# A GRU, two attentions and a mixture of experts on one core: gate inputs formed inside the recurrence, expert results stored by token and choice

## The reference

```python
def cell(h, x):                       # GRU, run over 512 steps for 4 sequences
    gi = x @ W_ih + b_ih
    gh = h @ W_hh + b_hh
    i_r, i_z, i_n = jnp.split(gi, 3, axis=-1)
    h_r, h_z, h_n = jnp.split(gh, 3, axis=-1)
    r = sigmoid(i_r + h_r); z = sigmoid(i_z + h_z)
    n = tanh(i_n + r * h_n)
    h_new = (1.0 - z) * n + z * h
...
x = x + differential_attention(GRU(cond_2048, x))   # causal, then a filter over frequencies, RMS norm
x = x + moe(attention(modulated_norm(x, cond_2048)))
...
# moe, over all 2048 tokens as one list: 64 experts, 6 choices a token
topk_w, topk_idx = jax.lax.top_k(softmax(xf @ gate_w.T), 6)
# pos: place of a choice within its expert; choices with pos >= CAP = 128 are dropped
gx = xp[buf_tok]                                       # 64 experts x 128 slots x 512
g, u = jnp.split(gx @ gate_up_proj, 2, axis=-1)        # inner size 192
eo = (silu(g) * u) @ down_proj * buf_w
routed = zeros.at[buf_tok].add(eo)                     # sum over a token's kept choices
out = routed + silu(xf @ sg.T) * (xf @ su.T) @ sd.T
```

## Time and profile before

| | |
|---|---|
| median of 3 runs | 4338.63 us (4338.46 to 4352.77) |
| the profiled execution | 4372.42 us, span 4370.6 us |
| gate inputs | 0 to 193 us |
| recurrence | 193 to 2070 us |
| attentions and filter | 2070 to about 3520 us |
| routing | about 3520 to 3792 us |
| experts | 3792 to 4217 us |
| combination | 4217 to 4370.6 us |
| busy, share of the span | TensorE 85%, VectorE 52%, ScalarE 32%, GpSimd 12% |

### The profile page before, as it was taken

The page is one execution under the profiler, slowest core; times in us unless marked ns, Lnnn a source line. Parts: engine busy times, 40 slices in busy tenths (PEclk is TensorE's granted clock), DMA queues, the critical chain, the costliest instruction groups (busy, mean ns, idle before and its releaser), DMA issues. The chain is left out here.

```text
span 4370.6 us, 166686 instructions
## 1 busy us (share of the span) xinstructions
PE 3724.0 (85%) x68215; PEld 2390.4 (55%) x68215; DVE 2284.5 (52%) x6296; ACT 1383.8 (32%) x4235; POOL 520.7 (12%) x1081
## 2 busy tenths in 40 slices
PE   8988888888888888888899999689999989688840
PEld 4477777777777777777344344244333344344420
DVE  2255555555555555555577777435666633222225
ACT  1133333333333333333344444224444411011100
POOL 0000000000000000000222222000000024200036
PEclk9999999999999999999999999899999889799975
DMA  3130000000000000000111110101211112278868
GB/s 102 48 136 0 0 0 0 0 0 0 0 0 0 0 0 0 0 0 6 61 52 43 41 50 17 70 29 52 67 50 50 52 68 72 66 251 265 265 200 203
DMA packets 136990, 253.11 MB, mean 58 GB/s; under 512 B 22135, under 2 KB 69379, under 8 KB 135012
## 3 DMA queue, kind: packets, MB, share of 16 engines
q1 hardware_dynamic: 97188, 157.86, 11.1%
q0 software_dynamic: 21056, 52.52, 4.3%
q10 hardware_dynamic: 18688, 41.96, 3.2%
HBM read 147.89 MB, written 62.92 MB: 48 GB/s over the span
## 5 line engine op out<-in xcount | busy, mean ns | idle before, releaser
L303 PE MATMUL gru_pr<-ahead,h 128*4 128x128 f32 x16384 | 556.7, 274 | 193.8 <-DVE h L384 193.8
L303 PEld LDWEIGHTS gru_pr<-ahead,h 128*4 128x4 f32 x16384 | 338.8, 88 | 399.7 <-DVE h L384 331.0
L303 PE MATMUL gru_pn<-ahead,h 128*32 128x128 f32 x16384 | 541.8, 273 | 0.0
L303 PE MATMUL gru_pz<-ahead,h 128*4 128x128 f32 x16384 | 541.7, 273 | 0.0
L303 PEld LDWEIGHTS gru_pn<-ahead,h 128*32 128x32 f32 x16384 | 458.4, 110 | 1.4
L303 PEld LDWEIGHTS gru_pz<-ahead,h 128*4 128x4 f32 x16384 | 438.0, 87 | 8.8
L331 ACT ACTIVATE gru_rn<-gru_pre 128x16 f32<-128x16 f32 x512 | 119.6, 234 | 704.6 <-DVE gru_pre L366 704.6
L364 DVE STREAM_TRANSPOSE gru_tr<-gru_pr 128x128 f32<-128x128 f32 x512 | 162.2, 317 | 335.1 <-PE gru_pr L303 335.1
L279 POOL COPY gru_pick<-ident 128x4 f32 x512 | 95.9, 187 | 1651.3 <-PE gru_pz L294 1645.9
L883 DVE TENSOR_REDUCE da_mx<-da_ps 128x2 f32<-128x1024 f32 (+3 forms) x256 | 201.2, 817 | 132.5 <-PE da_ps L576 132.5
L377 DVE STREAM_TRANSPOSE gru_tz<-gru_pz 128x32 f32<-128x32 f32 (+1 forms) x1024 | 195.1, 229 | 119.1 <-PE gru_pz L303 119.1
(11 more groups left out here) (281 smaller groups left out, 5418.8 us busy)
## 6 DMA issues: line engine op xcount, KB each, us to landing
ahead<-in_L_ffn_gate_up_proj SPq DMA_DIRECT2D x64, 768.0 KB, 9.2
ex_wd<-in_L_ffn_down_proj ACTq DMA_DIRECT2D x64, 384.0 KB
xg<-gru_zeros SPq DMA_DIRECT2D x4, 4096.0 KB
ex_xg<-xg ACTq DMA_DIRECT2D x64, 256.0 KB
eo<-ex_eo POOLq DMA_DIRECT2D x64, 256.0 KB
ahead<-wide SPq DMA_DIRECT2D x15, 1024.0 KB
ahead<-xnT SPq DMA_DIRECT2D x15, 1024.0 KB
da_wg<-ahead SPq DMA_DIRECT2D x45, 256.0 KB
```

The source lines that it names most:

```text
L303: last = nc.tensor.matmul(rows(j), of(c), whh[:, c, g, j, :], start=(c == 0 and start), stop=(c == KD - 1))
```

## The change

The inputs of the r and n gates are formed in the first stage for the first 32 time steps only (8 column groups of 4 products, 128x128). The others are formed within the recurrence: in each step but the last 32, TensorE does one 128x128 product for the block of 32 steps that follows, between the bias of n and the wait for h. Four such products are one column group; VectorE adds the bias and moves it to `giT` ahead of every fourth step, and GpSimd copies the group's columns of `W_ih` to a tile of its own, `wst`. `x` is kept transposed in `wide`, where each step's h takes the place of the inputs already used, and the second sequence is no longer held back for `W_ih`. The attention's weights come in the last 32 steps.

Each row of `xg` becomes 528 wide: beside the token's 512 values it carries the number of the token's first choice and its 6 experts; an empty slot has a million there. In the expert stage VectorE finds from these the row `token * 6 + choice` of each slot, and GpSimd stores the expert's rows to these places of a new tensor `yk` (12288 rows, cleared beforehand) with an indirect transfer, which leaves out empty slots. The combination then loads a tile's 6 rows a token, 12 KB in one piece for a partition, with plain transfers on SyncE's and ScalarE's queues in turn; it has no gather.

```diff
+                    transpose_x(b, k)
+            pe.wait_ge(w_spread, 3 * KD)
+            pe.wait_ge(xT_ready, B * KD)
+            for c in range(NG):
+                if c >= 2:
+                    pe.wait_ge(gi_out, c - 1)
+                for k in range(KD):
+                    last = nc.tensor.matmul(pg[:, c % 2, 0:B * 32], wih[:, k, c * P:(c + 1) * P], xT[:, k, :, 0:32], start=(k == 0), stop=(k == KD - 1))
                 last.then_inc(gi_psum, 1)
-
-            pe.wait_ge(ident_in, 16)
-            for k in range(KD):
-                transpose_x(0, k)
-            pe.wait_ge(w_spread, 3 * KD)
-            for b in range(B):
-                pe.wait_ge(xT_ready, (b + 1) * KD)
-                for c in range(NG):
-                    gate(b, c)
-                    if b < B - 1 and c in (3, 4, 5, 6):
-                        transpose_x(b + 1, c - 3)
...
+            sp.wait_ge(zero_set, 2)
+            R = 16
+            xg = t.xg_dram.rearrange("(n r p) d -> n p r d", r=R, p=P)
+            for n in range(SLOTS // (R * P)):
+                sp.dma_start(xg[n], zeros[:].broadcast_to([P, R, XW])).then_inc(cleared, 16)
+            yk = t.yk_dram.rearrange("(n r p) d -> n p r d", r=R, p=P)
+            for n in range(CHOICES // (R * P)):
+                sp.dma_start(yk[n], zeros[:, :, 0:D].broadcast_to([P, R, D])).then_inc(cleared, 16)
+            sp.wait_ge(cleared, 16 * (SLOTS // (R * P) + CHOICES // (R * P)))
+
+            sp.wait_ge(gi_psum, (NBL - 1) * NG)
...
+            with pool.Fori(0, NBL - 1) as kb:
+                block_of_z(kb)
+                with pool.Fori(0, NG) as c:
+                    for k in range(KD):
+                        if k == 2:
+                            pool.wait_ge(gi_out, kb * NG + c + 1)
+                            nc.gpsimd.tensor_copy(wst[:], wih[:, :, bass.ds(c * P, P)]).then_inc(wst_ready, 1)
+                        pick_step(kb, c * KD + k, k)
...
+            def next_gate_input(kb, c, k):
+                if k == 0:
+                    pe.wait_ge(gi_out, kb * NG + c + 1)
+                    pe.wait_ge(wst_ready, kb * NG + c + 1)
+                last = nc.tensor.matmul(pgi[:, 0:P], wst[:, k, :], xT[:, k, :, bass.ds(kb * 32 + 32, 32)],
+                                        start=(k == 0), stop=(k == KD - 1))
+                if k == KD - 1:
+                    last.then_inc(gi_psum, 1)
+
+            with pe.Fori(0, NBL - 1) as kb:
+                with pe.Fori(0, NG) as c:
+                    for k in range(KD):
+                        s = kb * 32 + c * KD + k
+                        add_z_input(s, k % 2)
+                        add_bias(s)
+                        next_gate_input(kb, c, k)
+                        step(s, k % 2)
...
+            def move_gate_input(kb, c):
+                dve.wait_ge(gi_psum, kb * NG + c + 1)
+                nc.vector.tensor_tensor(t.giT[:, bass.ds(kb * 32 + 32, 32), bass.ds(c * B, B)], pgi[:, 0:P].rearrange("p (b t) -> p t b", b=B),
+                                        t.gi_bias[:, 0, bass.ds(c, 1)].unsqueeze(2).broadcast_to([P, 32, B]), ALU.add).then_inc(gi_out, 1)
+
+            with dve.Fori(0, NBL - 1) as kb:
+                with dve.Fori(0, NG) as c:
+                    for k in range(KD):
+                        if k == 0:
+                            dve.wait_ge(gi_out, kb * NG + 1)
+                        if k == KD - 1:
+                            move_gate_input(kb, c)
+                        step(kb * 32 + c * KD + k, k % 2)
...
+                nc.vector.tensor_copy(yb[:, y, :, D], base[:]).then_inc(S["noted"], 1)
+                nc.vector.tensor_copy(yb[:, y, :, D + 1:D + 1 + K], ef[:].rearrange(k24, k=K)).then_inc(S["noted"], 1)
+                dve.wait_ge(S["noted"], b * 2 + 2)
+                nc.vector.tensor_scalar(base[:], base[:], float(K * T), None, ALU.add).then_inc(S["base_set"], 1)
+                dve.wait_ge(S["base_set"], b * 1 + (TT + 2))
...
+                    wait(pool, dest_ready, q, u + 1)
                     wait(pool, eo_ready, q, u + 1)
-                    nc.gpsimd.dma_start(t.eo_dram[bass.ds((q * U + u) * CAP, CAP), :], eo[:, u % 2, :]).then_inc(stored[u % 2], 16)
+                    pool.sem_inc(tick, 1)
+                    nc.gpsimd.indirect_dma_start(
+                        out=t.yk_dram, out_offset=bass.IndirectOffsetOnAxis(ap=dest[:, u:u + 1], axis=0),
+                        in_=eo[:, u % 2, :], in_offset=None, bounds_check=CHOICES - 1, oob_is_err=False).then_inc(stored[u % 2], 16)
...
+            def destinations(q, u):
+
+                v = u % U
+                wait(dve, ecur_set, q, u + 1)
+                nc.vector.scalar_tensor_tensor(hit[:], xg[:, v, D + 1:D + 1 + K], ecur[:, 0:1], kvec[:], op0=ALU.is_equal, op1=ALU.mult).then_inc(hit_done, 1)
+                wait(dve, hit_done, q, u + 1)
+                nc.vector.tensor_reduce(nth[:], hit[:], AX, ALU.add).then_inc(nth_done, 1)
+                nc.vector.tensor_scalar(ecur[:], ecur[:], 1.0, None, ALU.add).then_inc(ecur_set, 1)
+                wait(dve, nth_done, q, u + 1)
+                nc.vector.tensor_tensor(dest[:, v:v + 1], xg[:, v, D:D + 1], nth[:], ALU.add).then_inc(dest_ready, 1)
...
+        def loads_and_stores(queue, turn):
+            def load(n):
+                queue.dma_start(got[:, n % R, :, :].rearrange("p k d -> p (k d)"), rows[n]).then_inc(loaded[n % R], 16)
+
+            for n in range(turn, R, 2):
+                load(n)
+            for n in range(turn, NTILE, 2):
+                queue.wait_ge(summed, n + 1)
+                if n + R < NTILE:
+                    load(n + R)
+                queue.dma_start(out_t[n * P:(n + 1) * P, :], acc[:, n % R, :]).then_inc(stored[n % R], 16)
```

More of the change, by code:

```diff
@@ L30 @@
 SLOTS = E * CAP
+XW = D + 16
+CHOICES = B * T * K
 I = 192
@@ L183, in spread_w @@
                                               src.rearrange("p (j c i) -> p c j i", c=KD, j=KD)).then_inc(w_spread, 1)
-            for k in range(KD):
-                copy_x(0, k)
-            for k in range(KD):
-                spread_w(k)
+            for b in range(B):
+                for k in range(KD):
+                    copy_x(b, k)
+                    if b == 0:
+                        spread_w(k)
             dve.wait_ge(b_in, 16 * (4 * KD))
@@ L323, in _, with step @@
             act.wait_ge(set_up, 6)
-            with act.Fori(0, T) as s:
+            def step(s, kb):
                 gi = t.giT[:, bass.ds(s, 1), :].rearrange("p o c -> p (o c)")
+                act.wait_ge(gi_out, kb * NG + 1)
                 nc.scalar.activation(rn[:, :, 3], gi[:, ST:2 * ST], ACT.Copy).then_inc(gin_ready, 1)
@@ L336, in _ @@
                     nc.scalar.activation(cb(d1[:, part.start * B:part.stop * B, 2]), tz[:, part, 0:B], ACT.Sigmoid).then_inc(z_act, 1)
+            with act.Fori(0, NBL) as kb:
+                with act.Fori(0, 32) as n:
+                    step(kb * 32 + n, kb)
         @block.vector
@@ L1815, in _ @@
             nc.vector.tensor_copy(before[:], lf[:]).then_inc(S["ready"], 1)
+            nc.vector.tensor_reduce(above[:], lf[:], AX, ALU.add).then_inc(S["above_done"], 1)
+            dve.wait_ge(S["above_done"], 1)
+            for tt in range(TT):
+                nc.vector.tensor_scalar(base[:, tt:tt + 1], above[:], -float(K), float(K * (tt * P + P - 1)), ALU.mult, ALU.add).then_inc(S["base_set"], 1)
+            nc.vector.memset(yb[:, :, :, D:XW], 0.0).then_inc(S["base_set"], 1)
+            dve.wait_ge(S["base_set"], TT + 1)
             for k in range(KD):
@@ L2078, in round_of @@
                         copy_x(q, u + 1, first)
+                        if not first or u == U - 1:
+                            v = (u + 1) % U
+                            dve.wait_ge(stored[v % 2], q * (16 * U // 2) + (16 * ((u + 1) // 2 + 1) - 16 * U // 2))
+                        destinations(q, u + 1)
                     if not first or u:
@@ L2129, in _ @@
                     dve.wait_ge(stored[n % R], 16 * (n // R))
+                dve.wait_ge(loaded[n % R], 16 * (n // R + 1))
                 src = t.x1[:, n, :]
                 for k in range(K):
-                    dve.wait_ge(gathered[n % R][k], 16 * (n // R + 1))
                     if k:
```

144 lines of the change are left out of this document (65 added, 79 removed).

## The result

The changed kernel takes 4226.99 us (median of 4 runs, 4223.8 to 4241.51) against 4338.55 us before: ratio 0.9743, interval 0.9718 to 0.9768, 112 us faster. I had forecast 4183 us, 156 us faster, with a range of 4145 to 4240: the time lies in the whole range and outside the forecast's own, 4160 to 4205. The profiled execution has a span of 4227.2 us.

The account below looks back on a forecast made before the run. Bounds differed by stage: TensorE in gate inputs and the recurrence's closed chain, DMA largely in experts, GpSimd's indirect transfers in the combination. Terms -97 + 5 + 4 - 15 - 53 = -156 us gave 4183; own range 4160 to 4205, whole 4145 to 4240.

Parts of the forecast that it names:

- Gate inputs, -97: First stage: z inputs start at about 40 us in place of 137.8, 97 us less; ends -90 and -102.
- Recurrence, the product hidden: Each step's full-width product, 0.45 to 0.52 us, fits TensorE's 0.55 us pause before h; without cover 216 us.
- the small things: Recurrence loop: +5 us allowed for the product and all small things; other end +48 us.
- Rival 1: Recurrence: the full-width product doesn't fit in the pause, 0.10 us a step, 48 us, giving 4231 us; 14%.
- rival 2: Recurrence: GpSimd's copies to `wst` stop a VectorE scan, 120 x 0.32 = 38 us, giving 4221 us; 9%.
- Routing, +4: Routing stage: VectorE's small operations and waits before slots are written, plus setting up, add 4 us; ends +1 and +7.
- Experts, -15: Expert stage: fewer stored rows relieve DMA, new small operations stay hidden, 15 us less; ends -31 and +10.
- Rival 5: Expert stage: indirect stores cost there what the combination's gather did, 43 us, giving 4241 us; 3%.
- Combination, -53: Combination: plain loads replace gathers, VectorE's sums set the pace, 94 us in place of 147, 53 us less.
- rival 3: Combination: bound by DMA at 249 GB/s, 28 us more than forecast, giving 4211 us; 12%.

Follow-up runs that it names:

- g_twice: Changed kernel with each recurrence step's full-width product issued twice, the extra one to a PSUM bank nobody reads: 4334.39 us, ratio 0.9922.
- g_none: Changed kernel without the recurrence's full-width product, TensorE only counting, so later r and n inputs are wrong: 4224.91 us, ratio 0.9718.
- e_early: Changed kernel with the experts' loads released and waited for one by one, slot loads moved to SyncE's queue: 4158.18 us, ratio 0.9520.
- e_oob: Changed kernel with the indirect store's bound set to 0, so hardly any expert rows are stored: 4239.73 us, ratio 0.9754.

## Why the prediction was right and wrong

The change is faster, by 112 us for 156, and the two large gains came about as worked out. That the time lies in the whole range is in part luck: the range was that wide for rivals 1 to 3, none of which happened, and the 44 us that are missing come mostly from the experts (35 us off) and the recurrence (11 us off), neither by a mechanism that those rivals name.

**Gate inputs, -97: right**, -94. The z inputs start 2.6 us later than worked out, since TensorE waited for the last load of x until 30.46 us, for the 28 worked out. SyncE's 16 small issues ahead of the third load were not in the working.

**Recurrence, the product hidden: right, and the small things mis-sized**, +16 for +5. The sum 0.45 to 0.52 us against a pause of 0.55 is measured at 0.41, where TensorE comes late, against 0.44, and `g_twice` shows that hardly anything is left. Rival 1 is out: no usual step is longer. That a margin of 0.03 us, for the 0.03 to 0.10 worked out, held in every usual step was luck more than working. The move and the copy to `wst` (rival 2) cost nothing in any place of a group. What I hadn't listed are the loops. The inner loop's end holds TensorE for 0.25 us and so uses up the pause at the 14 turns from one block of 32 steps to the next, 0.4 us each, 5.5 us. `g_none` gives all of that back, but its second loop begins 1.6 us later still, so its recurrence is only 4.3 us shorter. The first three steps are together 6.4 us longer, and where the second loop begins 5 us more go; the three come to 17 us, which is the whole of the +16. In both places TensorE stood still waiting for nothing the profile shows (3.50 us at 121.11, 3.77 at 1877.07; 4.11 at 1873.44 in `g_none`) while the DMA engines were full with the clearing (356 GB/s from 110 to 130 us) or the attention's weights. The DMA queues of after, 1868 to 1882 us (packets, MB, share of 16 engines):

```profile
q1 hardware_dynamic: 1677, 3.04, 100.9%
q8 instruction: 2, 0.03, 1.2%
```

Two packets of instructions moved among 1677 others. That TensorE waits for instructions that queue behind these is argued, not tested.

**Routing, +4: not resolved.** 229 and 257 us occur with the same code, which hides a few us. It may also explain most of the 34 us by which the profiled execution of before lay over its median: that execution had the long one, and what its other runs had was not profiled. I took the whole difference of two profiles' stages as the change's, which it isn't: -112, not -143.

**Experts, -15: wrong**, +20. The failed step is to take the middle between the 24 / 0.78 = 31 us that go if DMA alone sets the stage and nothing. DMA's 0.78 was no sign of a limit: with the loads released earlier `e_early` reaches 0.95. What ended last were TensorE's waits for loads released late, which I read as room for a gain from fewer bytes. The chain from the output product over the load's landing to the next transpositions doesn't get shorter by fewer stored bytes: in `e_oob`, with hardly any, TensorE waits 72.6 us for loads and the stage takes 432. On top, with the indirect store the waits come more often in pairs of 2.2 and 0 us, and TensorE's clock falls: 424 us, 399 with the plain store, 392 with the waits filled. I had looked at TensorE's clock nowhere in this stage. Of the +20 us part may be chance, as profiles of one expert code differ by 10 to 14 us; -15 is excluded by all five profiles of the new code (415 to 429). Rival 5 had the place and came within 14 us of the time (4241), with the wrong mechanism: no rows need be written for the loss. How the store causes the pairs is open; its issue is 0.98 us in place of 0.54, and I tried neither a delay of the plain store nor another queue.

**Combination, -53: right**, -61. A sum takes 0.78 us for the 0.83 of the earlier trace rows, which is 5 of the 8 us, and the pace is VectorE's, at 316 GB/s over the stretch; rival 3, 249 GB/s, is out.

The measured differences without the routing's sum to -94 + 16 + 3 + 20 - 61 = -116 us; the runs give -112 and, the second time, -115.

## What to carry to other kernels

A DMA share of 0.8 with a compute engine that waits for loads can be late release rather than rate: look at what stands between a buffer's last reader and the load that refills it, before counting bytes. Release each buffer after its own last reader and wait for each load where it is first needed; the two were changed together here, for 100 us of the stage. And where TensorE waits in uneven portions, compare its granted clock first: filling the waits with idle products made the stage 32 us shorter, with no other change.

## What was not expected of the hardware

- Products that nobody reads, done while TensorE would wait, make the stage shorter: 424 to 392 us, the granted clock from 0.88 to 1.00.
- A full-width product of two records between products in tiles of 32 columns takes 0.41 us of TensorE from its start to the next tiled product, and two of them take 0.64 (502.78 to 503.42).
- GpSimd's copy of 128x512 at 1003.54 lay over VectorE's addition of two SBUF operands, which still started 0.46 us after its transposition and took 0.18. So it was with 118 of the 120 copies (GpSimd's times are rough), and the steps without a copy look the same; the scans of the earlier trace rows were held 0.23 us by the like.
- The routing stage takes 229 or about 257 us with the same instructions; what decides is open.
